# The beginning of a graph and expert kernel: pass count read behind the last unit, low one-hots split over two engines, adjacency cleared by two engines

## The reference, cut to what matters

```python
def gnn(H, W, bias, edge_row, edge_col, edge_val):
    msgs = edge_val[:, None] * (H @ W)[edge_col]
    out = jax.ops.segment_sum(msgs, edge_row, num_segments=1024)
    return relu(out + bias)

x = x + gnn(layernorm(x), W, bias, src, dst, edge_weight)
x = x + ffn(layernorm(x)[None], ...)[0]
```

## Time and profile before

| | us |
|---|---|
| median of 3 runs (451.71 to 453.12) | 451.98 |
| the profiled execution | 451.02 |
| its span, first to last instruction | 449.1 |
| TensorE busy | 389.5 (87%) |
| VectorE busy | 210.9 (47%) |
| GpSimd busy | 176.4 (39%) |
| ScalarE busy | 158.5 (35%) |

### The profile page before, as it was taken

One profiled execution on the slowest core, in us unless ns is written; L12 is line 12 of the kernel. 1 busy time (PEld: TensorE's weight loads), 2 busy tenths in 40 slices (PEclk: granted clock), 3 DMA queues, 4 the chain that ended last, 5 costly groups with the idle time before them and its releaser, 6 DMA issues.

```text
span 449.1 us, 6470 instructions
## 1 busy us (share of the span) xinstructions
PE 389.5 (87%) x1875; PEld 205.5 (46%) x1876; DVE 210.9 (47%) x669; ACT 158.5 (35%) x405; POOL 176.4 (39%) x275
## 2 busy tenths in 40 slices
PE   5789999899999998989999999997898789688800
PEld 4467776756656556433443444343333334334400
DVE  8799898325665767532323332331331321321136
ACT  4588999413232220322332333232312212213200
POOL 5579787313656554731323332331221221310100
PEclk9899999999999998999999999998999989999965
DMA  7999500130002673889999999999999999997169
GB/s 263 224 370 406 226 0 1 41 121 25 24 24 58 271 254 107 216 288 408 405 407 406 409 404 408 406 406 407 409 406 407 405 408 403 405 403 296 49 224 340
DMA packets 41349, 125.09 MB, mean 279 GB/s; under 512 B 7905, under 2 KB 8481, under 8 KB 41058
## 3 DMA queue, kind: packets, MB, share of 16 engines
q1 hardware_dynamic: 35522, 116.25, 68.5%
q0 software_dynamic: 5792, 8.43, 5.3%
HBM read 119.64 MB, written 13.91 MB: 297 GB/s over the span
## 4 chain that ended last, share of the span: by engine, by line
PE 70%; DVE 8%; issue 8%; POOL 5%; DMA 5%; ACT 1%; DVEq 1%; SPq 0%; POOLq 0%; ACTq 0%
PE bank L1380 24%; PE bank L1248 12%; PE bank L1410 12%; PE bank L1402 4%; PE bank L1197 4%; PE bank L1371 3%; PE bank L1166 3%; DMA A<-nx_rows,A 3%; PE bank L1236 2%; PE bank L1269 1%; DMA w<-totals 1%; POOL slots L500 1%; DVE stats L758 1%; POOL M L468 1%; POOL AT L468 1%
## 5 line engine op out<-in xcount | busy, mean ns | idle before, releaser
L1063 DVE SCALAR_TENSOR_TENSOR osl<-bank,b13T,osl 128x64 f32<-128x64 f32 x128 | 27.5, 277 | 156.9 <-ACT osl L689 156.9
L1380 PE MATMUL bank<-w,xhT 128*64 128x512 f32 x352 | 85.1, 627 | 13.3 <-issue 12.1
L682 ACT COPY xh<-bank 128x512 f32<-128x512 f32 x33 | 19.4, 587 | 144.0 <-PE bank L1380 140.7
L1248 PE MATMUL bank<-HW,AT 128*128 128x512 f32 x128 | 58.2, 593 | 0.0
L1380 PEld LDWEIGHTS bank<-w,xhT 128*64 128x64 f32 x352 | 26.3, 143 | 57.2 <-issue 54.6
L559 POOL DMA_INDIRECT totals<-GW,A x16 | 16.0, 1001 | 88.4 <-PE bank L1371 69.4
L559 POOL DMA_INDIRECT totals<-osl,A x17 | 17.0, 1001 | 79.2 <-PE bank L1371 59.7
L1410 PE MATMUL bank<-w,osl 128*64 128x512 f32 x176 | 41.8, 593 | 0.0
L603 ACT ACTIVATE osl<-iota,eT 128x128 f32<-128x128 f32 x120 | 36.7, 389 | 10.1 <-PE bank L1197 9.0
L555 POOL DMA_INDIRECT A<-nx_rows,A x33 | 34.6, 1047 | 12.2 <-issue 9.6
L1248 PEld LDWEIGHTS bank<-HW,AT 128*128 128x128 f32 x128 | 22.9, 191 | 21.0 <-issue 21.0
(11 more groups left out here) (223 smaller groups left out, 574.9 us busy)
## 6 DMA issues: line engine op xcount, KB each, us to landing
w<-in_L_ffn_W_dram SPq DMA_DIRECT2D x66, 1024.0 KB, 19.3
A<-in_L_ffn_W_dram SPq DMA_DIRECT2D x15, 1024.0 KB, 19.4
HW<-in_L_ffn_W_dram SPq DMA_DIRECT2D x10, 1024.0 KB, 18.3
AT<-in_L_ffn_W_dram SPq DMA_DIRECT2D x5, 1024.0 KB, 20.2
w<-totals SPq DMA_DIRECT2D x8, 512.0 KB, 7.2
out_dram<-X SPq DMA_DIRECT2D x8, 256.0 KB, 5.9
X<-in_x_dram SPq DMA_DIRECT2D x3, 512.0 KB, 8.7
w<-in_L_ffn_W_dram SPq DMA_DIRECT2D x3, 512.0 KB, 17.0
```

The costliest lines, as they stand in the source:

```text
L1063: ins = v.scalar_tensor_tensor(hT[b][:, m, CAP * h:CAP * h + CAP], bank[4][:, (HC + m) * P + CAP * h:(HC + m) * P + CAP * h + CAP], b13T[: ...
L1248: ins = t.matmul(bank[4 + s % 2][:, :], AT[:, s % 2, k, :], HW[:, k, :], start=(k == 0), stop=(k == NB - 1))
L1380: ins = t.matmul(bank[2 + b][CAP * h:CAP * h + CAP, :], xe[b][:, c, CAP * h:CAP * h + CAP], up_w[v][:, h, :, c, :], start=(c == 0), stop=( ...
```

## The change

- `R1` is read by all four engines behind their last pair instead of ahead of the first (on TensorE behind the first eight transposes of the gates' rows).
- Low one-hots: ScalarE builds tiles 0 to 5 of a group, VectorE tiles 6 and 7 in one instruction (`low_pair`), with a semaphore of its own, `osl_pair`, that TensorE waits for too. The window's column is loaded ahead of these waits.
- The copies `xhT` of all blocks are ScalarE's (`x_transposed`).
- A is cleared by VectorE (2400 words) and ScalarE (5920). GpSimd clears none of it and fills the sentinel there instead. The sentinel is 410 words a partition instead of 2050, and the DMA reads it five times.
- The clears of the first two banks stand ahead of the first one-hots and no longer behind quad 0's.
- The matmul that broadcasts the bases stands in the middle of block 0's product. Four spare transposes ahead of it are gone; two are added ahead of block 0 and eight ahead of the experts.
- Of the sixteen transposes of the gates' rows eight stand behind the first transpose of A.

```diff
-A_DVE, A_POOL = 2400, 5300
+A_DVE = 2400
+SENT, SENT_W = 5, 410
+OSL_A = 6
...
-            sp.dma_start(slots.rearrange("(p n) r -> p (n r)", p=P), sentinel).then_inc(sentinel_out, 16)
+            sp.dma_start(slots.rearrange("(p s n) r -> p s (n r)", p=P, s=SENT),
+                         sentinel.unsqueeze(1).broadcast_to([P, SENT, SENT_W])).then_inc(sentinel_out, 16)
...
-            g.memset(A[:, A_DVE:A_POOL], 0.0).then_inc(a_chain, 1)
+            g.memset(sentinel, NOWHERE).then_inc(consts, 1)
...
-            g.memset(sentinel, NOWHERE).then_inc(consts, 1)
...
-            a.memzero(A[:, A_POOL:]).then_inc(a_chain, 1)
+            a.memzero(A[:, A_DVE:]).then_inc(a_chain, 2)
...
-                for k in range(8):
+                for k in range(OSL_A):
                     ins = a.activation(osl[:, h % 2, k, :], iota[:, :], ACT.Abs, bias=eT[:, 1, ds(j * 32 + 8 * h + k, 1)])
...
+            def x_transposed(g, u):
+                act.wait_ge(xhT_ps, g + 1)
+                a.copy(xhT[:, u, :, :].rearrange("p c n -> p (c n)"), bank[4 + u][:, :]).then_inc(xhT_ready, 1)
...
                     x_times_w(j * 2 + u, u)
+                    if not (last and u):
+                        x_transposed(j * 2 + u + 1, 1 - u)
...
+            def low_pair(j, h):
+                v.scalar_tensor_tensor(osl[:, h % 2, OSL_A:8, :], iota[:, :].unsqueeze(1).broadcast_to([P, 8 - OSL_A, P]), -1.0,
+                                       eT[:, 1, ds(j * 32 + 8 * h + OSL_A, 8 - OSL_A)].unsqueeze(2).broadcast_to([P, 8 - OSL_A, P]),
+                                       ALU.mult, ALU.is_equal).then_inc(osl_pair, 1)
...
-                    if with_x and q % 4 == 3 and not (last and u):
-                        transposed_rows(b + 1, 1 - u)
+                    if q % 2 == 0 and not (with_x and first and q < 4):
+                        low_pair(j, q // 2)
...
+            gate_rows(wg_g, bank[6]).then_inc(raw_transposed, 1)
+            R1 = pe.value_load(rounds_sb[0:1, 0:1], min_val=1, max_val=N // WIN)
...
             transpose_a(0)
+            gate_rows(b_b13[0:1], bank[7])
+            gate_rows(b_b13[1:3], bank[7][:, 256:512]).then_inc(raw_transposed, 1)
...
-            keep_busy(bank[0], 20)
+            keep_busy(bank[0], 28)
```

More of the change, by code:

```diff
@@ L623, in _ @@
             act.wait_ge(slo_ready, 1)
-            for k in range(8):
+            for k in range(OSL_A):
                 ins = a.activation(osl[:, 0, k, :], iota[:, :], ACT.Abs, bias=eT[:, 1, k:k + 1])
-                if k == 3:
-                    act.wait_ge(xhT_ps, 1)
-                    a.copy(xhT[:, 0, :, :].rearrange("p c n -> p (c n)"), bank[4][:, :]).then_inc(xhT_ready, 1)
+                if k == 2:
+                    x_transposed(0, 0)
             ins.then_inc(osl_chain, 1)
             act.wait_ge(osl_chain, 1)
-            a.activation(osl[:, 0, :, :], osl[:, 0, :, :], ACT.Relu, scale=-1.0, bias=1.0).then_inc(osl_ready, 1)
-            act.wait_ge(edges_ready, 1)
-            R1 = act.value_load(rounds_sb[0:1, 0:1], min_val=1, max_val=N // WIN)
+            a.activation(osl[:, 0, 0:OSL_A, :], osl[:, 0, 0:OSL_A, :], ACT.Relu, scale=-1.0, bias=1.0).then_inc(osl_ready, 1)
             pair(0, True, False)
@@ L824, in _ @@
             dve.wait_ge(slo_ready, 1)
+            need(c_clear)
+            v.memset(bank[0][:, 0:QW], 0.0).then_inc(zeroed, 1)
+            for h in range(2):
+                low_pair(0, h)
             dve.wait_ge(base_ps, 1)
             v.tensor_tensor(eT[:, 0, :], eT[:, 0, :], bank[1][:, 384:512], ALU.add).then_inc(edges_ready, 1)
+            v.memset(bank[1][:, 0:QW], 0.0).then_inc(zeroed, 3)
             dve.wait_ge(edges_ready, 1)
-            R1 = dve.value_load(rounds_sb[0:1, 0:1], min_val=1, max_val=N // WIN)
             BEHIND = 3
@@ L1165, in x_product @@
                 for c in range(DC):
+                    if isinstance(g, int) and g == 0 and c == DC // 2:
+                        pe.wait_ge(base_ready, 1)
+                        t.matmul(bank[1][:, 384:512], ones[0:1, :], neg_base, start=True, stop=True).then_inc(base_ps, 1)
                     ins = t.matmul(bank[6 + u][:, :], xhT[:, u, c, :], GW[:, c, :], start=(c == 0), stop=(c == DC - 1))
@@ L1169, in _ @@
             x_rows(0, 0)
-            keep_busy(bank[7], 4)
-            pe.wait_ge(base_ready, 1)
-            t.matmul(bank[1][:, 384:512], ones[0:1, :], neg_base, start=True, stop=True).then_inc(base_ps, 1)
             x_product(0, 0)
@@ L1192, in pair @@
                             min_val=0, max_val=QW - TW, skip_runtime_bounds_check_because="DVE bounded them by min, and a tile's window starts after its quad's")
+                        if q % 2 == 0:
+                            pe.wait_ge(osl_ready, half + (q // 2 + 1))
+                            pe.wait_ge(osl_pair, half + (q // 2 + 1))
                         pe.wait_ge(m_pool, quad + (q + 1))
```

45 lines of the change are left out of this document (16 added, 29 removed).

## The result

The changed kernel takes 445.67 us (445.4 to 446.04) against 451.85 us (451.41 to 453.12) of the kernel before, measured beside each other. The ratio is 0.986, with a 95% interval of 0.984 to 0.988. The prediction was 445.5. A second series of the same kernel gave 446.25 us (443.51 to 447.28) and 0.987 (0.984 to 0.991). The profiled execution of after took 446.04 us with a span of 443.9; that of before 451.02 with 449.1. The spans differ by 5.2, the medians by 6.2 us.

The account below looks back on a forecast made before the run. The beginning was taken as bound by arithmetic and waits between engines, the experts' loop near its end by weights. Terms 4.1 + 2.6 + 0.2 - 0.4 = 6.5 us gave 445.5 against the median of 451.98; forecast range 442.8 to 447.0 (0.62).

Parts of the forecast that it names:

- Up to the first quad: Part 1, start to first quad: shorter memsets, moved reads and clears bring the first addition to A 4.1 us earlier.
- Pair 0: Part 2, first addition to pair 1: copy moved to ScalarE saves 0.6, a low pair costs 0.35; about nothing.
- Together about nothing: Pair 0's net: VectorE's saved copy against its added low pairs, no gain or loss.
- its 7.1 us without a pause: VectorE's stretch in pair 0, first addition to normalising of block 2, 21.44 to 28.56 us.
- Pairs 1 to 3: Part 3: ScalarE's smaller groups close one hole of 0.93 us per pair; gain 2.6 us, bounds 0 and 2.8.
- Its rival: VectorE takes ScalarE's place in pairs 1 to 3, a pair stays near 16 us, no gain there: 448.1, chance 0.14.
- The end: Part 4, around the adjacency's first transpose: eight gates' transposes moved behind it gain 0.2 us, bounds -0.6 to 0.8.
- Ahead of the experts: Part 5: eight more spare transposes before the experts' rows lose 0.4 us, between 0 and 1.6.
- One to one to the end: From ahead of the experts' loop to the kernel's end: a gain there reaches the end in full.
- The rival by which the gain does not arrive: Experts' loop fed by a stream that began earlier, hiding the beginning: time 452, chance 0.03.
- The clock rival: TensorE's clock drops early, slowing block 0's product before the first quad: costs 1.5 to 2.4 us, 447.5, chance 0.12.
- The port rival: VectorE's low pairs wait for GpSimd's tiles reading SBUF: 454 at a full tile of 0.81 us, chance 0.04.

Follow-up runs that it names:

- after, again: The changed kernel once more, unchanged, in a second series: 446.25 us (443.51 to 447.28), ratio 0.987 to the kernel before.
- f1: Changed kernel with four of each eight low one-hots on VectorE instead of two, four on ScalarE: median 2.2 us slower than the changed kernel.
- e7: Changed kernel with all sixteen transposes of the gates' rows ahead of the adjacency's transposes again: 447.1 us.
- e6: Changed kernel with 20 spare transposes ahead of the first experts' rows instead of 28: 445.5 us.
- e1: Kernel before with the clears alone: GpSimd's share of A to ScalarE, sentinel a fifth as long and earlier: 3.0 us less than the kernel before.
- f2: Changed kernel with the register load of quad 1's place made together with that of quad 0: 443.8 us.
- e2: Changed kernel with the old clears: GpSimd clears part of A again, whole sentinel's memset beside block 0's normalising: 4.2 us more than the changed kernel.
- f3: Changed kernel with quad 1's load early, eight low one-hots on ScalarE in pair 0, eight spare transposes before block 0's product: 443.36 us, 0.983 to before.
- e5: Changed kernel with the window's register load behind the waits for low one-hots; pairs 1 to 3 take 45.4 us, whole time not in the text.
- e8: Changed kernel with fewer early spare transposes, 2 instead of 14 and none instead of 8: 1.8 us longer than the changed kernel.

## Why the prediction was right, and where its terms were off

The median was hit to 0.2 us, but that is better than the terms deserve. Against the profiled execution the sum was 6.5 us and 5.2 came out: 4.0 up to the first addition, a loss of 1.4 in pair 0, 3.0 in pairs 1 to 3, 0.3 at the end of the sums, a loss of 0.25 ahead of the experts and of 0.5 at the very end. Errors of both signs cancelled in part, and the median moved 1 us more than the profiled executions did. That part is luck; the second series gave 446.25.

1. **Up to the first quad: right.** Predicted and measured: block 0 ready 7.9 and 8.1; the first edge operation shorter by 0.8 and 0.7 (0.93 to 0.23; block 0's rows start 0.63 earlier); W landed 9.9 and 10.3; addition to the edge table ends 12.9 and 13.1; first one-hots 13.3 and 13.47; quad 0 16.0 and 15.63; first addition 17.3 and 17.41. The low pair was put at 0.35; alone it takes 0.41, and two in a row 0.73. What the part did not see is that 4.1 us is one execution's number. Before, half clock from 12.8 us on the earlier trace rows was part of it, and in after it lies elsewhere; after, again has 2.9 us. In a single pair of traces this is luck as well.
2. **Pair 0: the step that failed.** "Together about nothing" was 1.4 us of loss in the profiled execution and nothing in the other (13.2 us from the first addition to pair 1, as before). The count of instructions was right. But the sum has no term for VectorE's register loads: its 7.1 us without a pause hold loads of 0.3 us, and the one at 19.2 us took 1.8. With the pause that this made, the 7.1 us became 8.0, and 6.8 in after, again. A row to see it by was there: TensorE's loads in the kernel before, of which those at 18.3 and 20.0 us took 1.1 and 1.15 us, while VectorE's stood at 16.0 and 23.8. The change moved one of VectorE's into that stretch.

```profile
L1190 PEldq TENSOR_LOAD <-wrow x32: 327/332/1147, 18.3 to 80.7; - x32
```

3. **Pairs 1 to 3: right in mechanism, a little small.** 2.6 predicted, 3.0 measured: the three holes were 1.0 to 1.1 us each and not 0.93, and 0.3 is still lost in the first unit. VectorE, at 14.3 busy us in a pair as predicted (47.2 to 62.2 us), kept up. Its rival took place only in f1, weaker than priced.
4. **The end:** from the last quad's end to the first messages' product it is 4.55 us instead of 4.86, about as predicted (0.2). The adjacency's first transpose came another 0.3 earlier, but that much goes to the eight transposes behind it. e7 prices the alternative at 0.3.
5. **Ahead of the experts:** 0.25 us lost in the trace for 0.4 predicted, and by its time e6 finds nothing. The traces show a little more: the experts' rows are transposed 4.0 to 4.3 us behind the first spare transpose with twenty (e1, before, e6), and 4.8 in seven of the eleven traces with 28. In f2, the only one whose 28 ran at full clock throughout, it is 4.1, and TensorE waited 0.85 us for the rows behind them.
6. **One to one to the end: not quite.** 0.5 us went between the adjacency's first transpose and the experts' product, as said under 4 and 5, and 0.5 in the last 26 us, where VectorE waits 0.67 us for a load at 430.5 us for which it waited 0.41 before. The experts' loop itself moved by 5.7 us as a whole: its last spare transpose starts at 417.6 instead of 423.3. From the first experts' product to that one the fourteen executions take 243.3 to 244.2 us, and from there to the end 25.5 to 26.7, in no order that the edits explain. The rival by which the gain does not arrive falls.
7. **The clock rival** (0.12) did not come in either profile of after, and came in e7's with the same code up to there: one-hots 1.6 us late, and 447.1 against the 447.5 put on it, of which about 0.3 is e7's own edit.
8. **The port rival** falls: VectorE's memset-long wait is real for a sentinel's memset (2.01 against 0.52 us, e1 and e2), but 32 low groups, most of them beside GpSimd's tiles, took 0.41 and 0.68 us with no more than 0.17 on top. What the rival had wrong is who waits: GpSimd's tiles got longer, by up to 0.57 us in f1, and it had the room. The Trainium skill, "SBUF — State Buffer", section "Who interferes with whom", would have the loser wait for a whole instruction; these traces agree for VectorE beside the memset and for GpSimd's tiles that start inside a VectorE instruction, and not for VectorE's low groups beside tiles.

## To carry to other kernels

Moving work off an engine that is late in one stage onto one that has slack there is paid in the stages where the second engine is the chain: here six and two won 1.5 us in pairs 1 to 3 and lost most of it ahead of them. A split made stage by stage is the way to keep both; f3, which has it among its edits, is the shortest of the traces. A long memset on another engine deserves a look before any arithmetic does, since it showed only as one slow instruction elsewhere. And before a term is read from one trace, see where half clock lay in it.

## What the runs showed of the hardware

- Register loads take 0.30 us on VectorE and 0.33 on TensorE (medians, 32 of each). Of those that start between about 15 and 21 us here some take 0.8 to 1.8, on either engine, in a different place in each execution, and others the usual 0.3 (VectorE's at 19.7 us in f1: 0.32). The DMA engines are full then (share 1.0), but so they are at 31 to 47 us, where the loads take 0.3; what differs is that they move 187 GB/s in the first stretch and 407 in the second (after). The cause is open. An instruction fetch, which stood beside the long load in after (19.2 us), is not it: in e6 the load at 19.2 us took 1.26 and the next fetch came at 24.6.
- GpSimd's one-hot tiles (0.79 us) that start while VectorE is inside an instruction on SBUF take longer by about the rest of it, up to 1.35 us in f1; VectorE beside a tile loses 0.17 us at most. Beside a GpSimd memset VectorE's normalising took 2.01 us instead of 0.52 to 0.55.
- Half clock fell on a different stretch ahead of 160 us from execution to execution, also of the same kernel, and on none in e5, f1 and f3; in e2 and e6 it came into work whose only pause in some 20 us was one of 0.3 us, about 2 us earlier. It costs 1.6 us where TensorE is the bound (3.61 against 1.98 for four matmuls), and about 0.2 in pair 0 of after and nothing in that of after, again, where the quads wait for VectorE (an estimate from the lengths of the pair). A pause of 1.56 us in TensorE was followed by it in e7, one of 1.44 in after was not.
- In e8 the granted clock reads 1.00 while every matmul ahead of 19 us takes the time of the lower level; the records of the clock begin only at 19.3 us there.
